# Long TensorE pieces divided into two or four parts, placed between the score matmuls of a fused transformer block

## The reference

```python
x = x + attention0(layernorm(x))      # 16 heads of 8, softmax, biases on q, k, v
x = x + ffn0(layernorm(x))            # (silu(gate) * up) @ down, hidden 384, int weights / 127
x = x + attention1(layernorm(x))      # qkv projection, RMS-normalised q and k, softmax, projection
x = x + ffn1(layernorm(x))            # x @ base + bias + LoRA experts weighted by a softmax router
```

## Time and profile before

| | before |
|---|---|
| median of 3 runs | 2164.41 us (2163.48 to 2167.84) |
| span of the profiled execution | 2165.0 us |
| TensorE busy | 1980.4 us, 91% |
| VectorE busy | 1638.9 us, 76% |
| ScalarE busy | 1431.8 us, 66% |
| GpSimd busy | 434.7 us, 20% |
| mean granted TensorE clock | 0.957 |
| chain that ended last | TensorE 62%, issue 15%, VectorE 10%, DMA 5% |

### The profile page before, as it was taken

How to read it: one execution, slowest core, us unless ns; L and a number is a source line. 1 busy time by engine, 2 the same in 40 slices (tenths; PEclk the granted TensorE clock), 3 DMA queues, 4 the chain that set the end, 5 groups by cost and what they waited for, 6 DMA issues and landing times.

```text
span 2165.0 us, 38228 instructions
## 1 busy us (share of the span) xinstructions
PE 1980.4 (91%) x10706; PEld 763.2 (35%) x10706; DVE 1638.9 (76%) x3602; ACT 1431.8 (66%) x2921; POOL 434.7 (20%) x571
## 2 busy tenths in 40 slices
PE   3958999999999999999999999999999999999785
PEld 1223333333333333333333333333333333333332
DVE  5638888787887878778787877878787778888471
ACT  2615676676766767676776767677676767676643
POOL 2112121131212113121211312121121213121200
PEclk8858999999999999999999999999999999999977
DMA  5112314040311404031130404114050412302020
GB/s 108 55 25 58 87 34 122 18 135 19 111 44 39 116 17 137 17 116 39 46 109 17 138 16 119 36 46 109 17 138 17 118 36 62 94 20 72 18 63 16
DMA packets 162656, 140.94 MB, mean 65 GB/s; under 512 B 38761, under 2 KB 144050, under 8 KB 162482
## 3 DMA queue, kind: packets, MB, share of 16 engines
q1 hardware_dynamic: 162482, 139.29, 23.2%
HBM read 77.38 MB, written 55.57 MB: 61 GB/s over the span
## 4 chain that ended last, share of the span: by engine, by line
PE 62%; issue 15%; DVE 10%; DMA 5%; POOL 4%; ACT 2%; SPq 2%; DVEq 0%; POOLq 0%; ACTq 0%
PE ps L1159 17%; PE ps L1134 14%; PE ps L1144 14%; DVE neg_max L881 5%; PE ps L1209 4%; PE ps L1110 3%; PE ps L1173 3%; PE ps L1182 2%; PE ps L1214 2%; DMA k_stack<-k_rows 2%; ACT probs L661 1%; DVE bn L858 1%; DMA k_rows<-kp 1%; PE ps L1221 1%; DMA rden_all<-rden_rows 1%
## 5 line engine op out<-in xcount | busy, mean ns | idle before, releaser
L881 DVE TENSOR_REDUCE neg_max<-ps 128x1 f32<-128x512 f32 x2048 | 1323.5, 681 | 231.2 <-PE ps L1134 194.0
L661 ACT ACTIVATE probs<-ps 128x512 f32<-128x512 f32 x2048 | 1093.8, 599 | 347.2 <-PE ps L1144 345.6
L1134 PE MATMUL ps<-k_stack,q_stack 96*128 96x512 bf16 x2048 | 798.7, 392 | 80.2 <-DVE neg_max L881 51.2
L1144 PE MATMUL ps<-q_stack,k_stack 128*128 128x512 bf16 x2048 | 782.7, 385 | 16.8 <-ACT probs L661 14.0
L1159 PE MATMUL ps<-probs,v_aug 128*32 128x512 f32 x4096 | 548.8, 608 | 0.4
L1144 PEld LDWEIGHTS ps<-q_stack,k_stack 128*128 128x128 bf16 x2048 | 202.9, 100 | 441.8 <-ACT probs L661 244.9
L1134 PEld LDWEIGHTS ps<-k_stack,q_stack 96*128 96x128 bf16 x2048 | 202.3, 99 | 371.7 <-DVE neg_max L881 192.4
L561 POOL TENSOR_TENSOR o_raw<-o_raw,rden_all 128x512 f32<-128x512 f32 x64 | 81.4, 1272 | 580.7 <-DMA rden_all<-rden_rows 580.7
L1159 PEld LDWEIGHTS ps<-probs,v_aug 128*32 128x32 f32 x4096 | 80.7, 108 | 184.4 <-ACT probs L661 102.3
L667 ACT ACTIVATE xn<-x,shift,rstd 128x128 f32<-128x128 f32 x192 | 80.7, 486 | 49.4 <-POOL shift L544 49.3
L578 POOL TENSOR_TENSOR ht<-up,gs 128x512 f32<-128x512 f32 x48 | 60.9, 1268 | 257.3 <-ACT up L642 257.3
(11 more groups left out here) (109 smaller groups left out, 1487.5 us busy)
## 6 DMA issues: line engine op xcount, KB each, us to landing
q_stack<-q_rows SPq DMA_DIRECT2D x128, 192.0 KB, 3.4
k_stack<-k_rows SPq DMA_DIRECT2D x128, 192.0 KB, 4.3
rden_all<-rden_rows SPq DMA_DIRECT2D x64, 256.0 KB
q_rows<-qp SPq DMA_DIRECT2D x32, 384.0 KB, 2.6
k_rows<-kp SPq DMA_DIRECT2D x32, 384.0 KB, 3.0
q_rows<-qp SPq DMA_DIRECT2D x32, 256.0 KB, 2.9
k_rows<-kp SPq DMA_DIRECT2D x32, 256.0 KB, 3.0
x_in<-in_L_attn_x SPq DMA_DIRECT2D x16, 256.0 KB, 2.8
```

The lines of the kernel that those rows point to most:

```text
L661: act.activation(probs[:, u % RING, :], ps[:, bank_of(l, u), :], ACT.Exp).then_inc(exps, 1)
L881: dve.tensor_reduce(neg_max[l][:, pair // 2, col:col + 1], ps[:, BANKS + bank_of(l, n), :], AX.X, ALU.max, negate=True).then_inc(max_taken, 1)
L1134: pe.matmul(ps[:, BANKS + bank_of(l, 2 * n + e), :], q_stack[l][0:QROWS, pair, tok:tok + 128], k_stack[l][e][0:QROWS, pair, :], start=True ...
L1144: pe.matmul(ps[:, bank_of(l, u), :], k_stack[l][e][:, pair, tok:tok + 128], q_stack[l][:, pair, :], start=True, stop=True).then_inc(scores, 1)
```

## The change

Each long piece gets a number of parts in a table. The list of what stands in a slot is now one of quarter places q, two behind each half step: a piece with one part stands where it stood (behind h = 2·step + 1), one with two parts has the first behind h = 2·step and the second behind 2·step + 1, one with four has two parts behind each. Part 0 does the waits of the whole piece; the last part signals that it is written. Single matmuls of 512 columns (q0, k0, gate, up) become two of 256 columns with the same weights; the others are cut by token tiles. The scores and their order are the same. On VectorE, the adds behind pr1, pr0 and dn move one half step later, and so do the statistics and moments of layer norms 1 and 2.

```diff
+PARTS_OF = {"q0": 2, "k0": 2, "v0": 2, "v1": 2, "rt": 2, "pr0": 4, "pr1": 4, "dn": 4, "out": 4, "qka": 2, "qkb": 2,
+            "g0": 2, "u0": 2, "g1": 2, "u1": 2, "g2": 2, "u2": 2}
+def sub_slots(name, at_step):
+    n = PARTS_OF[name] if name in PARTS_OF else 1
+    first = {1: 3, 2: 1, 4: 0}[n]
+    return [(4 * at_step + first + (4 // n) * k, k, k == n - 1) for k in range(n)]
...
-                            if h == 23:
+                            if h == 24:
                                 project_add(1, x3, i - 2)
...
-                            if h == 19:
+                            if h == 20:
                                 project_add(0, x1, i)
-                            if h == 20:
+                            if h == 21:
                                 dve.wait_ge(read["pr0"], i + 1)
                                 stats(1, x1, i)
-                            if h == 21:
+                            if h == 22:
                                 moments(1, i)
                                 factors_in(1, i)
...
-                            if h == 43:
+                            if h == 44:
                                 down_add(i)
-                            if h == 44:
+                            if h == 45:
                                 dve.wait_ge(read["dn"], i + 1)
                                 stats(2, x2, i)
-                            if h == 45:
+                            if h == 46:
                                 moments(2, i)
                                 factors_in(2, i)
...
+            def by_column(w, xt, half):
+                return pe.matmul(gen[:, 256 * half:256 * half + 256], w, xt[:, 256 * half:256 * half + 256],
+                                 start=True, stop=True)
...
-            def piece(name, i, at, kind, b):
+            def piece(name, k, i, at, kind, b):
                 before = piece_before(kind, at, name)
-                if before is not None:
+                if k == 0 and before is not None:
                     pe.wait_ge(read[sem_name(before[0])], count(before[0], i + before[1]))
...
                 elif name[0] in "gu":
-                    pe.wait_ge(read["xt1"], b + 1)
+                    if k == 0:
+                        pe.wait_ge(read["xt1"], b + 1)
                     w = w_gate if name[0] == "g" else w_up
-                    last = pe.matmul(gen, w[:, int(name[1]), :], xnt[1][:, :], start=True, stop=True)
+                    last = by_column(w[:, int(name[1]), :], xnt[1], k)
                 elif name == "dn":
-                    pe.wait_ge(ht_done, NH * (b + 1))
-                    for t in range(TT):
-                        for c in range(NH):
-                            last = pe.matmul(gen4[:, t, :], ht[:, c, 128 * t:128 * t + 128], w_down[:, c, :],
-                                             start=c == 0, stop=c == NH - 1)
+                    if k == 0:
+                        pe.wait_ge(ht_done, NH * (b + 1))
+                    for c in range(NH):
+                        last = pe.matmul(gen4[:, k, :], ht[:, c, 128 * k:128 * k + 128], w_down[:, c, :],
+                                         start=c == 0, stop=c == NH - 1)
...
-                    if s == 1 and "At" in have:
+                    if h == 3 and "At" in have:
                         attend_pv(past[0], UNITS - 4, past[1])
-                    if s % 2 and s > 1 and "A" in have:
-                        attend_pv(now[0], 2 * s - 6, now[1])
-                    for at_step, name in pieces:
-                        if at_step == s:
-                            piece(name, i, at, kind, i + PIECE[name][0])
+                    if h % 4 == 3 and h > 3 and "A" in have:
+                        attend_pv(now[0], h - 7, now[1])
+                    for q in (2 * h, 2 * h + 1):
+                        if q in plan:
+                            name, k, last = plan[q]
+                            op = piece(name, k, i, at, kind, i + PIECE[name][0])
+                            if last:
+                                op.then_inc(written[sem_name(name)], 1)
```

More of the change, by code:

```diff
@@ L1168, in turn_norm, with by_token @@
                 return last
-            def by_token(dst, xt, w, more=None):
-                for t in range(TT):
+            def by_token(dst, xt, w, tiles, more=None):
+                for t in tiles:
                     last = pe.matmul(dst[:, t, :], xt[:, 128 * t:128 * t + 128], w, start=True, stop=more is None)
@@ L1192, in piece @@
                 elif name in ("q0", "k0"):
-                    pe.wait_ge(read["xt0"], b + 1)
-                    last = pe.matmul(gen, (wq if name == "q0" else wk)[:, :], xnt[0][:, :], start=True, stop=True)
+                    if k == 0:
+                        pe.wait_ge(read["xt0"], b + 1)
+                    last = by_column((wq if name == "q0" else wk)[:, :], xnt[0], k)
                 elif name == "v0":
-                    pe.wait_ge(read["xt0"], b + 1)
-                    last = by_token(gen4, xnt[0], wv[:, :])
+                    if k == 0:
+                        pe.wait_ge(read["xt0"], b + 1)
+                    last = by_token(gen4, xnt[0], wv[:, :], (2 * k, 2 * k + 1))
                 elif name == "v1":
-                    last = by_token(gen4, xnt[2], wqkv[:, 256:384])
+                    last = by_token(gen4, xnt[2], wqkv[:, 256:384], (2 * k, 2 * k + 1))
                 elif name[0] == "m":
@@ L1204, in piece @@
                 elif name in ("pr0", "pr1"):
-                    last = project(int(name[2]), b)
+                    l = int(name[2])
+                    if k == 0:
+                        pe.wait_ge(att_ready[l], 2 * b + 2)
+                    last = project(l, k)
                 elif name[0] in "gu":
-                    pe.wait_ge(read["xt1"], b + 1)
+                    if k == 0:
+                        pe.wait_ge(read["xt1"], b + 1)
                     w = w_gate if name[0] == "g" else w_up
-                    last = pe.matmul(gen, w[:, int(name[1]), :], xnt[1][:, :], start=True, stop=True)
+                    last = by_column(w[:, int(name[1]), :], xnt[1], k)
                 elif name == "dn":
-                    pe.wait_ge(ht_done, NH * (b + 1))
-                    for t in range(TT):
-                        for c in range(NH):
-                            last = pe.matmul(gen4[:, t, :], ht[:, c, 128 * t:128 * t + 128], w_down[:, c, :],
-                                             start=c == 0, stop=c == NH - 1)
-                elif name in ("qka", "qkb"):
-                    pe.wait_ge(read["xt2"], b + 1)
-                    half = int(name == "qkb")
-                    for t in (0, 1):
-                        tok = 128 * (2 * half + t)
-                        last = pe.matmul(gen[:, 256 * t:256 * t + 256], xnt[2][:, tok:tok + 128], wqkv[:, 0:256],
-                                         start=True, stop=True)
+                    if k == 0:
+                        pe.wait_ge(ht_done, NH * (b + 1))
+                    for c in range(NH):
+                        last = pe.matmul(gen4[:, k, :], ht[:, c, 128 * k:128 * k + 128], w_down[:, c, :],
+                                         start=c == 0, stop=c == NH - 1)
+                elif name in ("qka", "qkb"):
+                    if k == 0:
+                        pe.wait_ge(read["xt2"], b + 1)
+                    tok = 128 * (2 * int(name == "qkb") + k)
+                    last = pe.matmul(gen[:, 256 * k:256 * k + 256], xnt[2][:, tok:tok + 128], wqkv[:, 0:256],
+                                     start=True, stop=True)
                 elif name in ("qt", "kt"):
@@ L1228, in piece @@
                 elif name == "rt":
-                    pe.wait_ge(read["xt3"], b + 1)
-                    last = by_token(gen[:, 0:TT * 16].rearrange("p (t n) -> p t n", t=TT), xnt[3], w_mid[:, :])
+                    if k == 0:
+                        pe.wait_ge(read["xt3"], b + 1)
+                    last = by_token(gen[:, 0:TT * 16].rearrange("p (t n) -> p t n", t=TT), xnt[3], w_mid[:, :],
+                                    (2 * k, 2 * k + 1))
                 elif name == "ct":
@@ L1235, in piece @@
                 elif name == "out":
-                    last = by_token(gen4, xnt[3], w_base[:, :], more=(coef_t, w_lora[:, :]))
-                last.then_inc(written[sem_name(name)], 1)
+                    last = by_token(gen4, xnt[3], w_base[:, :], (k,), more=(coef_t, w_lora[:, :]))
+                return last
             def slot(kind, i, at):
@@ L1249, in slot @@
                             pe.wait_ge(read["k0"], 1)
-                            last = by_token(gen4, xnt[0], wv[:, :])
+                            last = by_token(gen4, xnt[0], wv[:, :], range(TT))
                         else:
```

27 lines of the change are left out of this document (13 added, 14 removed).

## The result

The changed kernel takes 2371.89 us (median of 4 runs, 2370.1 to 2380.45), the kernel before 2165.45 in the same comparison (2163.48 to 2167.84). The ratio is 1.096, 95% interval 1.093 to 1.098: slower by 206 us. The forecast was 2353, its range 2290 to 2388.

What follows compares the result with a forecast made beforehand. TensorE was taken to set the pace, so its waits are paid in full. Stalls, moved adds and switches, less a credit, gave 12.56 us per element, times 15 elements 188, added to 2165: 2353 us, range 2290 to 2388.

Steps and rivals of the forecast that it cites:

- The rule: At pieces sharing PSUM bank gen: stall is when the reader frees it minus when TensorE returns, 0.44 us after T.
- T: On TensorE's timeline, for each piece, the time at which the first score after it starts; readers are timed from it.
- The moved adds: VectorE's adds behind pr0, dn, pr1 start 0.98 us later; losses 0.91 to xt1, 0.74 to xt2, 0.98 to m02.
- The k_stack credit: Behind m02 TensorE waits for k_stack anyway, so m02 and k0 are partly paid from that wait: 0.53 us per element back.
- The loss from k0 to m02: On the way from pr1 to m02, which already waited for VectorE's add: the later add costs 0.98 us.
- qkb: Before qkb, TensorE waits for VectorE's take of qka, bank free at T + 1.20: 0.76 us stall.
- u2: Like u0 and u1, waits for VectorE's gate product, free at T + 1.57, TensorE back at 0.44: 1.13 us stall.
- The switches: More switches between kinds of matmul at 17 cut pieces per element: 0.08 us each, 1.36 per element, ends 0 and 2.9.
- Rival A: At the loop's edge and other waits: a quarter of the sum is given back because TensorE comes late; 2306 us, chance 0.13.
- Rival B: From g0 to dn: new stalls lower TensorE's clock, one such stretch more per element; 2383 us, chance 0.13.
- Rival C: Readers follow the earlier halves; even supply removes TensorE's 51.2 us of waits for maxima; 2134 us, chance 0.04.

Runs made afterwards that it cites:

- e8: Changed kernel, but the gate product squares tanh's output, so ScalarE's tanh releases gen; the gate's value is left out of the result: 2305.61 us.
- e5: Kernel before with only q0, v0 and v1 divided in two parts, adds not moved: 2166.55 us, ratio 0.9997.
- e3: Kernel before with no piece divided; only VectorE's adds, statistics and moments moved one half step later: 2206.11 us, ratio 1.0185.
- e6: Changed kernel, all 17 pieces divided, but VectorE's adds, statistics and moments stay one half step earlier, where they were: 2318.71 us, ratio 1.070.
- e9: Changed kernel with one VectorE instruction moved: the cast of a quarter's maxima stands behind the take of qka instead of ahead: 2347.2 us, ratio 1.0835.
- e1: Kernel before with only u0, u1 and u2 divided in two parts, adds not moved: 2227.2 us, ratio 1.028.
- e7: Changed kernel with qka and qkb undivided, all else as there: 2330.03 us, ratio 1.0755.

## Why the prediction was right, and where a term was off

- **The rule was right.** Free at the distance of the reader from T, TensorE back after one pair: u at T + 1.57, xt1 at T + 7.94 (7.90 by the steps), g0 at T + 0.98 behind the copy (0.85 forecast), g1 at T + 0.86, dn at T + 2.26, pr0 at T + 2.71 (2.61). e8 changed the reader and left the halves, and the stall followed the reader. e5 divided three pieces around which no reader is late, and nothing was lost.
- **The moved adds were right**: 0.91, 0.74 and 0.98 forecast, 0.92, 0.76 and 0.96 in e3. The k_stack credit was 0.47 to 0.56, forecast 0.53. The loss from k0 to m02 was 0.3 smaller than forecast; with pr1 divided but the add unmoved (e6) this way is 0.2 shorter than before.
- **qkb was mis-sized**: "the maximum of the score pair between the halves now comes about 0.25 later, so I take free at T + 1.20". With the take ahead of the cast it is T + 1.17 (e9), so this part was right. Left out was the cast itself, which now stands between T and the take: T + 1.38 where it takes 0.17, and 0.8 to 1.1 later where it starts behind GpSimd's product. I costed the readers by their own durations and not by what runs on GpSimd beside them. With the low clock the collision cost 1.29 us per element (5.26 on the mean against 3.97), 19 us. That is as much as the forecast was short by, and the other errors cancel; that they do is luck.

The trace of before held the same collision at two other places, each once per iteration. At one nobody waited: VectorE had 0.88 us to spare before its next add. The kernel before, the subtraction behind a cast on VectorE, and GpSimd at that time:

```profile
1075.51 1.05 DVE L896 TENSOR_TENSOR neg_max<-neg_max,neg_high 128x16 f32<-128x16 f32 x1
```

```profile
1075.38 1.16 POOL L555 TENSOR_TENSOR qp<-qf,qp 128x512 bf16<-128x512 f32 x1 [1.79 <-ACT qp L642]
```

At the other TensorE did wait, behind g2. The kernel before, a factor of a layer norm (0.17 us elsewhere) and the maximum behind it, GpSimd, and the wait of TensorE:

```profile
1021.76 1.00 DVE L872 TENSOR_SCALAR neg_mean<-mv 128x4 f32<-128x4 f32 x1
...
1022.74 0.68 DVE L881 TENSOR_REDUCE neg_max<-ps 128x1 f32<-128x512 f32 x1
```

```profile
1021.46 1.27 POOL L578 TENSOR_TENSOR ht<-up,gs 128x512 f32<-128x512 f32 x1 [3.46 <-ACT up L642]
```

```profile
1023.47 0.39 PE L1134 MATMUL ps<-k_stack,q_stack 96*128 96x512 bf16 x1 [0.33 <-DVE neg_max L881]
```

- **u2 was mis-sized the other way**, by that wait: u2 started at T + 2.46 before, not at T + 1.96 as u0 and u1, in all 13 repeats. In the changed kernel it starts at T + 1.59 like them, and the 0.5 is gone (0.76 more and not 1.21). The forecast gave all three u the full stall and no credit; that is 7 us. With g2 whole (e1) the stretched factor delays the gate product instead, u2 starts at T + 2.03, and it costs 1.20.
- **The switches** cost 0.00 (g), 0.09 (pr0) to 0.11 (u) per cut where the rows show them, within the bounds; 0.08 served.
- **Rival A** did not come: from m00 to q0 TensorE lost 0.22 more. The reason given against it held, since the pause is VectorE's own (2.8 to 3.1 in both). **Rival B** came in part, not between g0 and dn but behind qka, in 5 of 13 repeats, some 6 us of the sum (their mean of 6.19 us against 4.92 for the other six with a late cast, 5 x 1.26); without the collision (e9, e6, e7) it did not come, and with it not always (e8). **Rival C** fell: the shortest reader needed 0.85 us and VectorE's waiting more than doubled.

## What to carry to other kernels

Where pieces share one buffer, what counts is the time from the end of one to the start of the next, against the time its reader needs; dividing a piece so that it starts earlier and ends at the same place takes from that time, and gives nothing to the reader. Count per gap: free at T + reader, back at T + what stands between. Then look at what the other engines do beside each reader, since a stall makes an operation critical that had been hidden. The trace of before can show such a collision already: an operation that takes several times as long as the same one elsewhere.

## What the runs showed of the hardware that was not expected

- A VectorE cast of 128 x 16 numbers, 0.17 us alone, took up to 1.26 us when a GpSimd product of two SBUF tensors had started before it, and a tensor_scalar of 128 x 4 numbers 0.99 instead of 0.17; the maxima (one PSUM input) and the take of qka (one input in PSUM) kept their times beside it.
- A hardware loop's edge stopped VectorE 2.8 to 3.1 us in ten kernels and 1.7 to 2.0 in the four in which tanh and the gate product have exchanged semaphores, with about one instruction packet fewer per edge. Which part of that exchange does it is open. It was worth 24 to 29 us (1.1 to 1.3%) with every operation kept.
- The granted clock stayed at 1.00 through pauses of 0.3 to 1.0 us between matmuls, and fell in 5 of 11 stretches of the changed kernel where the cast made one pause 1.6 to 1.9 us long (0.72 and 0.88 in the two shown), but in none of 12 such stretches of e8. Behind the pause at the loop's edge it fell at 9 of 11 edges before; one fall cost some 1.5 to 1.8 us.
